# A graph convolution whose rows are gathered by step of the pipeline instead of by tile of edges

## The reference

```python
z   = concatenate([x[dst], x[src], edge_attr], axis=-1)
msg = sigmoid(z @ Wf.T + bf) * softplus(z @ Ws.T + bs)
agg = segment_sum(msg, dst, num_segments=n)
# then: normalise agg over the nodes, add x, layer norm, relu, add x, layer norm
```

## Time and profile before

| | |
|---|---|
| median of 3 runs | 3372.05 us |
| the profiled execution | 3374.32 us, span 3372.5 us |
| busy share of the span | PE 79%, DVE 64%, ACT 36%, POOL 69% |
| convolution's first gather to first statistics instruction | 2182.63 to 3263.28 us |
| mean granted TensorE clock | 0.92 of 2.4 GHz |

### The profile page before, as it was taken

The page is one execution under the profiler, slowest core; times in us unless marked ns, Lnnn a source line. Parts: engine busy times, 40 slices in busy tenths (PEclk is TensorE's granted clock), DMA queues, the critical chain, the costliest instruction groups (busy, mean ns, idle before and its releaser), DMA issues.

```text
span 3372.5 us, 69633 instructions
## 1 busy us (share of the span) xinstructions
PE 2658.0 (79%) x16221; PEld 1982.1 (59%) x16222; DVE 2142.3 (64%) x4942; ACT 1230.6 (36%) x1689; POOL 2340.1 (69%) x2392
## 2 busy tenths in 40 slices
PE   6599997775978776749877767788888888888874
PEld 6366555764755555647555566566666666666654
DVE  6755554657322234566554467588888888888886
ACT  2433332010000000110000002287888888888866
POOL 3677777775777777767777777477777777776710
PEclk8799999887999988879899979899999999999987
DMA  5344445334655552248777734444444444444411
GB/s 158 98 147 150 151 143 160 94 112 129 183 151 142 151 136 58 68 115 283 227 219 216 213 85 115 119 128 127 126 127 127 126 126 127 125 119 114 120 47 39
DMA packets 346022, 454.94 MB, mean 135 GB/s; under 512 B 135643, under 2 KB 260599, under 8 KB 342311
## 3 DMA queue, kind: packets, MB, share of 16 engines
q0 software_dynamic: 88624, 207.58, 22.6%
q10 hardware_dynamic: 127520, 197.33, 18.3%
q1 hardware_dynamic: 129768, 48.71, 5.9%
HBM read 357.03 MB, written 101.90 MB: 136 GB/s over the span
## 4 chain that ended last, share of the span: by engine, by line
POOL 41%; issue 20%; PE 18%; DVE 8%; DMA 8%; DVEq 2%; SPq 2%; ACT 1%; POOLq 0%; ACTq 0%
POOL shared L762 32%; POOL shared L797 9%; PE ps L964 6%; DMA shared<-q_dram,idx 6%; PE ps L955 3%; PE ps L1205 3%; PE ps L947 2%; SPq L637 1%; DVE work L2431 1%; DVE work L2440 1%; PE ps L1208 1%; ACT work L1540 1%; DVEq L2011 1%; PE ps L1224 1%; ACT work L1394 1%
## 5 line engine op out<-in xcount | busy, mean ns | idle before, releaser
L762 POOL DMA_INDIRECT shared<-y_even,idx x1056 | 1041.7, 986 | 357.6 <-issue 335.8
L797 POOL DMA_INDIRECT shared<-q_dram,idx x784 | 778.5, 993 | 295.5 <-issue 234.8
L955 PE MATMUL ps<-shared,work 128*128 x4368 | 661.1, 299 | 347.3 <-SPq L597 297.8
L955 PEld LDWEIGHTS ps<-shared,work 128*128 128x128 f32 x4368 | 595.1, 208 | 428.6 <-issue 417.7
L2135 DVE TENSOR_TENSOR acc<-acc,ps 128x129 f32 x546 | 156.2, 286 | 869.8 <-PE ps L955 770.0
L762 POOL DMA_INDIRECT shared<-y_odd,idx x528 | 509.2, 964 | 179.2 <-issue 160.6
L1205 PE MATMUL ps<-pq,work 128*128 x1664 | 502.4, 404 | 141.2 <-issue 95.2
L2431 DVE TENSOR_TENSOR work<-ps,shared 128x256 f32<-128x256 f32 x832 | 294.7, 416 | 172.6 <-PE ps L1208 145.6
L1205 PEld LDWEIGHTS ps<-pq,work 128*128 128x128 f32 x1664 | 259.2, 196 | 236.3 <-issue 166.2
L974 PE MATMUL ps<-pq,work 128*128 128x385 bf16 x1456 | 287.6, 346 | 42.3 <-DVE pq L2111 19.8
L1512 ACT ACTIVATE pq<-ps,blT_sb 128x512 f32<-128x512 f32 (+1 forms) x28 | 16.5, 631 | 696.5 <-PE ps L1142 696.5
(11 more groups left out here) (368 smaller groups left out, 3889.4 us busy)
## 6 DMA issues: line engine op xcount, KB each, us to landing
work<-counts_dram ACTq DMA_DIRECT2D x156, 384.0 KB
counts_dram<-work ACTq DMA_DIRECT2D x26, 1568.0 KB
ea_parts<-work ACTq DMA_DIRECT2D x128, 196.0 KB
ea_sb<-ea_parts SPq DMA_DIRECT2D x196, 128.0 KB
work<-counts_dram ACTq DMA_DIRECT2D x52, 416.0 KB
shared<-y_even,idx POOLq DMA_INDIRECT x1056
shared<-q_dram,idx POOLq DMA_INDIRECT x784
shared<-y_odd,idx POOLq DMA_INDIRECT x528
```

Source lines behind the costliest of these rows:

```text
L762: pool.indirect_dma_start(msg[:, u, 0:F], None, y_two[layer % 2], bass.IndirectOffsetOnAxis(ap=idx[:, u:u + 1], axis=0)).then_inc(s_quad[q ...
L797: pool.indirect_dma_start(q_ring[:, u * 2 * F:(u + 1) * 2 * F], None, q_dram, bass.IndirectOffsetOnAxis(ap=idx[:, u:u + 1], axis=0)).then_ ...
L955: last = te.matmul(ps[:, SUM_BANKS[i], 0:FA], lhsT=oh4[:, OH_SLOTS[i], u, :], rhs=shared[:, bass.ds(place + u * FA, FA)], start=u == 0, st ...
```

## The change

The gathers are made by pair instead of by tile. A table of sources by pair is made in the same way as the one of destinations (`src_pairs` beside `dlo`): seven more gathers in `conv_rows`, one more set of seven transposes on PE, two more copies on DVE. A ring slot then holds the four pairs of one step, so that step g uses slot g and nothing has to be looked up: POOL makes 208 x 4 = 832 gathers instead of 784, the ring has 8 slots, DVE adds the whole slot with one instruction of 1024 columns, and the waits count steps. The attributes of a slot are loaded with four DMAs of 128 columns, at tile numbers that SP reads from a table (one register load for each slot). The tables that gave slots and needed quads go, and with them their instructions. BELOW falls from three to two chunks of seven windows.

```diff
-RC = 7
+RC = 8
-CONV_TURNS = NQ // RC - 1
+CONV_TURNS = NG // RC
-        BELOW = 3 * CW
+        BELOW = 2 * CW
 # SP
-            def give_edges(q, at):
-                sp.dma_start(ea_sb[:, q * QT * P:(q + 1) * QT * P], ea_parts[:, bass.ds(at, QT * P)]).then_inc(s_ea[q], 16)
+            def give_edges(q, g):
+                sp.reg_load(tile_regs, regs[0:1, bass.ds(g * QT + NC * P, QT)])
+                for t, r in enumerate(tile_regs):
+                    sp.dma_start(ea_sb[:, (q * QT + t) * P:(q * QT + t + 1) * P],
+                                 ea_parts[:, bass.ds(sp.snap(r, min_val=0, max_val=(NT - 1) * P), P)]).then_inc(s_ea[q], 16)
...
-                    sp.wait_ge(s["added"], done_regs[q])
+                    sp.wait_ge(s["added"], m * (RC * G) + ((q + 1 - RC) * G + G * GB))
 # POOL
                 for c in range(NC):
                     pool.indirect_dma_start(d_rows[:, c * P:(c + 1) * P], None, dst_sorted, off).then_inc(s["rows"], 16)
+                    pool.indirect_dma_start(s_rows[:, c * P:(c + 1) * P], None, src_sorted, off).then_inc(s["rows"], 16)
...
-            with pool.Fori(0, NQ // RC) as m:
+            with pool.Fori(0, CONV_TURNS) as m:
 # PE
-                    w_of_pair, e_of_pair = load_pairs(g)
+                    w_of_pair = load_windows(g)
                     pe.wait_ge(s["oh_copied"], g + 3)
-                    pe.wait_ge(s["ea_landed"], quad_needed)
+                    pe.wait_ge(s["ea_landed"], g + 1)
...
-            for j in range(GB):
+            for j in range(RC):
                 conv_step(j, j)
-            with pe.Fori(1, NG // GB) as m:
+            with pe.Fori(1, CONV_TURNS) as m:
 # DVE, tables: L1955 to L1960 and L1965 to L1975 go; instead
+            link(v.tensor_scalar(tabf[:, 1, :], sch[:, TK, 0:NC], float(P), None, ALU.mult))
 # DVE, layer 0
                 last.then_inc(s["rowsf"], 1)
+                v.tensor_copy(s_rowsf, s_rows).then_inc(s["rowsf"], 1)
...
+                v.tensor_copy((dlo, src_pairs)[k][:, :], ps_tail.rearrange("p c e -> p (c e)")).then_inc(s["dlo_ready"], 1)
 # DVE, step
-                    slots = load_slots(g)
                     dve.wait_ge(s["pre_ready"], g + 5)
-                    dve.wait_ge(s["q_landed"], quad_needed)
+                    dve.wait_ge(s["q_landed"], g + 1)
...
-                    for t in range(G):
-                        last = v.tensor_tensor(pre[:, slot % 2, t, :], ps_pre[:, slot % 2, t, :],
-                                               q_ring[:, bass.ds(slots[t] * (2 * F), 2 * F)], ALU.add)
-                    last.then_inc(s["added"], G)
+                    mine = (slot - 2) % RC * QT * 2 * F
+                    v.tensor_tensor(pre[:, slot % 2, :, :], ps_pre[:, slot % 2, :, :],
+                                    q_ring[:, mine:mine + QT * 2 * F].rearrange("p (t f) -> p t f", f=2 * F), ALU.add).then_inc(s["added"], G)
 # DVE, end
-            for c in range(3):
+            for c in range(BELOW // CW):
                 add_beta(c)
```

More of the change, by code:

```diff
@@ L309, in build_gnn @@
         d_rowsf = work[:, 5376:6272]
-        s_rowsf = work[:, 8320:9216]
+        s_rowsf = work[:, 4480:5376]
         assert at[0] <= r_off and NC * P == 896
@@ L665, in _ @@
                 conv_quad(0, q, True, False)
[L667 to L675, removed]
+            with sp.Fori(1, CONV_TURNS - 1) as m:
                 for q in range(RC):
                     conv_quad(m, q, False, False)
-            needed(NQ // RC - 1)
             for q in range(RC):
-                conv_quad(NQ // RC - 1, q, False, True)
+                conv_quad(CONV_TURNS - 1, q, False, True)
             for q in (RC - 2, RC - 1):
-                sp.wait_ge(s_ea[q], NQ // RC * 16 + ea_given(q))
+                sp.wait_ge(s_ea[q], CONV_TURNS * (QT * 16) + ea_given(q))
                 sp.sem_inc(s["ea_landed"], 1)
-                sp.wait_ge(s_quad[q], NQ // RC * QT * 16 + SAGE_LANDED)
+                sp.wait_ge(s_quad[q], CONV_TURNS * (QT * 16) + SAGE_LANDED)
                 sp.sem_inc(s["q_landed"], 1)
@@ L1091, in sage_sums @@
                     for b in range(TAIL):
-                        both(b, columns_after if layer == 0 and b == 0 else None)
+                        both(b, columns_after(b) if layer == 0 and b < 2 else None)
                     for b in range(TAIL, DTURNS):
@@ L1207, in conv_step @@
                                   start=True, stop=False)
-                        last = te.matmul(o, lhsT=ea_sb[:, bass.ds(e_of_pair[t] * P, P)], rhs=we_rows[:, :],
+                        last = te.matmul(o, lhsT=ea_sb[:, ((slot - 1) % RC * QT + t) * P:((slot - 1) % RC * QT + t + 1) * P], rhs=we_rows[:, :],
                                          start=False, stop=True)
@@ L1214, in conv_step @@
                     for t in range(G):
-                        last = te.transpose(ps_ohT[:, t, :], oh[:, slot, t, :], ident[:, :])
+                        last = te.transpose(ps_ohT[:, t, :], oh[:, slot % GB, t, :], ident[:, :])
                     last.then_inc(s["oh_tr"], 1)
@@ L2329, in sage_adds @@
                     for b in range(TAIL):
-                        both(b, conv=not layer and b == 0)
+                        both(b, conv=not layer and b < 2)
                     for b in range(TAIL, DTURNS):
@@ L2452, in conv_step @@
                     v.tensor_tensor(mm[:, (slot - 3) % 2, :, :], gates[:, :, 0:F], gates[:, :, F:2 * F], ALU.mult).then_inc(s["msgd"], 1)
-            for j in range(GB):
+            for j in range(RC):
                 conv_step(j, j)
-            with dve.Fori(1, NG // GB) as m:
-                for g in range(GB):
-                    conv_step(m * GB + g, g)
+            with dve.Fori(1, CONV_TURNS) as m:
+                for g in range(RC):
+                    conv_step(m * RC + g, g)
             for j in range(NG, NG + GB):
-                conv_step(j, j % GB)
+                conv_step(j, j % RC)
             in_loop(0, 0, n_links)
@@ L2483, in _ @@
             dve.wait_ge(s["x_in"], NCH * 16 + 32)
-            for c in range(3, NCH):
+            for c in range(BELOW // CW, NCH):
                 add_beta(c)
```

134 lines of the change are left out of this document (48 added, 86 removed).

## The result

The changed kernel takes 3391.0 us, the median of 5 runs (3388.0 to 3393.3), against 3372.6 (3370.0 to 3375.5) of the kernel before run beside it: a ratio of 1.0052, 95% interval 1.0041 to 1.0063. It is slower by 18 us, which is the forecast case. The profiled execution is the fastest of the five, 3388.0 us with a span of 3386.2, so the traces differ by 13.7 us only.

A forecast was written before the change was run, and what follows sets the result against it. It took POOL's gathers as the convolution's bound early, the steps late. Convolution +23.4 (-28.4 + 207 d, d = 0.25), start -3.1, end +1.0 gave +21.3 on the profiled 3374.3 us: 3395.6, as median 3393, range 3352 to 3430.

The forecast's parts named there:

- the forecast case: Whole kernel: slower through POOL's 48 more gathers and the stalls, d over 0.18, 3379 up to 3441 us; chance 0.57.
- d: Convolution: POOL's time lost to stalled gathers per step, counted for 207 steps; taken as 0.25 us, between 0 and 0.49.
- Holding: Convolution gathers: stalls beside DVE's mult, 207 steps at 0.25 us, 51.8 us in all.
- two points, 0.37: Convolution: the mult can catch a gather at two points, 0.185 us each, 0.37 us a step together.
- Tail: Convolution's end, last gather to statistics: 39.5 us falls to 13.5, as steps then wait for gathers.
- Start: Before layer 0: DVE's tables shrink to about 0.6 us on a path where all later work waits, -3.1 us.
- End: After the statistics: one of three `add_beta` moves behind the wait for PE's sums, +1.0 us.
- What bounds the kernel now: Convolution before the change: POOL sets the pace early, 5.19 us a quad; the steps late, 5.10 us.
- Hidden, as said: SP's five DMAs, 3.4 to 4.6 us a slot, hide behind gathers; seven more `conv_rows` gathers, 8.8 us, in POOL's idle time.
- No difference: Whole kernel: rival with d between 0.115 and 0.18, today's 0.19 being next door; chance 0.14.
- Faster: Convolution: rival, the mult falls between a gather's points, d below 0.115; near 0 the time is 3342 us; chance 0.20.
- SP's case: Convolution: rival, SP becomes the bound if small DMAs cost 1.05 us each, 5.4 us a slot, 3427 us; chance 0.09.

The follow-up runs named there:

- the 54 gathers: Kernel before with 26 instead of 28 gathers in every turn of seven slots from the second on, 730 in all: 3372.4 us, ratio 0.9986.
- 782 gathers: Changed kernel with 30 instead of 32 gathers in every turn of eight slots from the second on: 3306.7 us, ratio 0.9804 to the kernel before.
- a relief of the steps that left the 784 gathers alone: Kernel before with PE's and DVE's loops in turns of eight steps and one PE register load a step less: 3347.6 us, ratio 0.9907.
- a relief that left PE idle longer in one place: Kernel before with PE's window registers kept and the quad numbers loaded once per four steps: 3377.8 us, ratio 1.0011.
- rows of quarters: Changed kernel with mult and one-hot each as four instructions of 128 columns: 3368.2 us, ratio 0.9987 to the kernel before.
- Doubling the work that can hold a gather: Changed kernel with the mult, or the one-hot, done a second time into spare columns: ratios 1.0069 and 1.0057 to the kernel before.

## Why the prediction was right, and where it was not

The forecast case held, d = (1079.5 - 831 x 1.25) / 207 = 0.197, over the 0.18 from which it decides. It held by 0.017 of d, with a largest term that was 11 us too high, so it was in part luck. From the first gather to the statistics it is 1094.5 us, where the prediction had about 1104. By terms, on the profiled executions:

- *Holding.* d was taken 0.25 and is 0.197: 11.0 us too much. The term was mis-sized in its working: it gave the mult two points in a gather and the one-hot none, and by "two points, 0.37" went above today's 0.19. The traces have one point and two instructions. In 208 steps 159 gathers are held (the mult holds 100, the one-hot 59), 0.76 a step, by 0.25 us on average (40.3 / 159), where the two points would make 2 x 0.68 / 1.25 = 1.09 a step by 0.34. That a place fixed by the landings raises d did not show either: 143 of the 159 are the second gather of their slot, and d is still today's 0.19.
- *Tail.* 13.5 taken, 15.0 measured. The last add starts 4.1 us after the last gather's start, where only the landing of 2.76 was counted: the gather's own 0.94 was forgotten.
- *Start.* -3.1 taken, -2.1 measured at the first gather. Where the other microsecond went was not followed.
- *End.* +1.0 taken, +1.9 measured. Up to L2428 it is 9.06 us against 8.08 before, and the row above shows that PE's sums end that wait, not the two `add_beta`, done at 3282.09. These sums take 8.78 us; before they took 7.79 (L1240). The granted clock is at its lower level until 5.1 us into them, before until 3.1. The price came out right there for a wrong reason; the rest comes later and was not followed.
- Together 21.3 - 11.0 + 1.5 + 1.0 + 0.9 = 13.7, the difference of the two traces.

*What bounds the kernel now* was read wrongly, though the sum does not show it. "It sets the pace", said of POOL in the early stretch, fell with the 54 gathers that were worth 5 us. POOL's 5.19 us a quad and the steps' 5.14 were both there, and the prediction took the busier-looking chain for the bound. The steps were the bound through the whole convolution. The sum stood because it compared the new floor with the measured 1041.2 + 39.5, whichever engine had set these. In truth the change made a larger gain and a larger loss than the text says: with 782 gathers its structure is 2.0% faster than the kernel before, 66 us, and 50 gathers take back 84.

*The stall.* "Caught at two points" by the mult was one point and two instructions. In the kernel before, too, the one-hot holds gathers, 108 against the mult's 78. With the reading that it does not falls the judgement on the Trainium skill, "SBUF — State Buffer", "Who interferes with whom": its rule, that a DVE instruction with two SBUF inputs contends with a GpSimd instruction that reads SBUF and one with at most one such input, outside the two-port modes, does not, agrees with every count above (one-hot and mult hold, the add, the combine and the sums, each with one input in PSUM, never). The gather at 2707.13 in the earlier trace rows looked undisturbed beside the one-hot because that one-hot began 0.48 us into it, past the point. And the gather at 2703.24 there was held by the one-hot: its mult starts at 2703.43, so the one-hot ended near 2703.51, and 0.82 us later the gather is over.

*Hidden, as said:* SP's five DMAs a slot (the rows of its waits show only landings, and POOL's idle time between gathers stays at (246.6 - 31.8 + 38.1 + 0.3) / 831 = 0.30 us each, the 31.8 being the wait before the first), and the doubled `conv_rows`. No run changed the attributes' loads; that the smaller rows cost nothing rests on these waits.

*The rivals.* "No difference" missed by 0.017 of d, 3.6 us. "Faster" needed the mult to fall clear of the gathers; with the mult cut to an eighth the kernel still only ties with the one before, since the one-hot remains. Two of the sums there are 1 to 2 us off: d = 0.49 gives 3443, not 3441, and SP's case 3426, not 3427.

## What to carry to other kernels

Where two engines' paces stand within a few per cent of each other, a chain of waits names one of them and not the price of relieving it; take a few per cent of work away from each in turn and see which one moves the time. Buying a faster step with more work on the engine next in line pays only up to the point where that engine takes over: here a relief of the steps that left the 784 gathers alone gave 31 us, and the one that came with 48 more gathers lost 18. Before the steps of two runs are compared, compare their granted clocks: a relief that left PE idle longer in one place lost by the clock what it had gained. Before a rule is dismissed by a row, ask whether in that row the two instructions met at the moment the rule speaks of.

## What the runs showed of the hardware

- A gather is held at one moment near its start, by a one-hot or mult (both inputs in SBUF) that began more than 0.03 us before it and ends at least 0.15 us into it: 159 of 159 times in the changed kernel, 186 of 186 in the one before. It then ends 0.82 us after the end of that instruction, against 0.95 for a whole gather. Of two or three such instructions of 0.68 us in a row, the next one does not hold it again; beside rows of quarters nine gathers were held to the row's end, up to 2.28 us.
- A one-hot or mult that began later in a gather neither held it nor took much longer itself: the longest of all in the changed kernel took 0.75 us, the median 0.68.
- Doubling the work that can hold a gather changed the holding little (40.1 us, then 38.7 and 43.2), since the gather behind a held one starts too late in the row to be held.
- A register load of four numbers with a stride took PE's sequencer 1.01 us, other loads 0.33.
- Behind idle times of PE of 1.0 to 2.7 us the granted clock fell to 1.2 of 2.4 GHz 11 times in the steps of the kernel before, and 4 to 40 times in the runs made from it. Two products that take 0.60 us then took 1.06, and a turn of four steps 1.4 to 1.7 us more.
